# A four-layer graph network on one core: unit and group bases by PE, key preparation ahead of the squares, a two-table start of twelve groups, and node phases with table rows by ACT

## The reference, cut to what matters

```python
def _L0_gnn_ref(x, rows, cols, vals):               # layer 0: hyperbolic weighted mean
    x_hyp = expmap0(x, C)
    x_hyp_agg = weighted_midpoint_spmm(x_hyp, C, rows, cols, vals)
    return logmap0(x_hyp_agg, C)
...
x = _layernorm(x + _L0_gnn_ref(x, src, dst, edge_weight), axis=-1)
x = _layernorm(x + _L1_gnn_ref(x, src, dst, ...), axis=-1)   # conv, 64 experts top 2, batch norm
x = _layernorm(x + _L2_gnn_ref(x, src, dst), axis=-1)        # sum over edges, scaled by degrees
x = _layernorm(x + _L3_gnn_ref(x, edge_index, ...), axis=-1) # sum over edges, two matmuls, residual
```

## Time and profile before

| | us |
| --- | --- |
| median of 3 runs | 7333.98 |
| lowest and highest | 7331.43, 7337.74 |
| the profiled execution, its own time | 7343.66 |
| its span in the trace | 7342.10 |

### The profile page before, as it was taken

One profiled execution on the slowest core, in us unless ns is written; L12 is line 12 of the kernel. 1 busy time (PEld: TensorE's weight loads), 2 busy tenths in 40 slices (PEclk: granted clock), 3 DMA queues, 4 the chain that ended last, 5 costly groups with the idle time before them and its releaser, 6 DMA issues. The chain is left out here.

```text
span 7342.1 us, 132036 instructions
## 1 busy us (share of the span) xinstructions
PE 5009.0 (68%) x33175; PEld 3585.0 (49%) x33176; DVE 3839.1 (52%) x17654; ACT 1973.7 (27%) x5480; POOL 5243.1 (71%) x4321
## 2 busy tenths in 40 slices
PE   1666666666666677608998744951499995799985
PEld 1555555555555555505655433840265553565554
DVE  6776666777777777563242365322633325324225
ACT  1233334444444445332111001320311111211103
POOL 1788888888888888827777766147677776677774
PEclk6898888888888888659999856975699996899997
DMA  9677777777766777567775412741556563555553
GB/s 220 72 75 69 70 75 79 82 87 90 91 98 99 101 102 106 70 205 246 234 233 190 149 43 68 208 120 46 158 183 196 187 194 99 187 183 195 186 167 89
DMA packets 941947, 982.32 MB, mean 134 GB/s; under 512 B 203011, under 2 KB 824681, under 8 KB 941536
## 3 DMA queue, kind: packets, MB, share of 16 engines
q0 software_dynamic: 310624, 275.22, 29.3%
q1 hardware_dynamic: 284610, 520.71, 22.3%
q10 hardware_dynamic: 346302, 181.56, 8.6%
HBM read 622.06 MB, written 337.58 MB: 131 GB/s over the span
## 5 line engine op out<-in xcount | busy, mean ns | idle before, releaser
L793 POOL DMA_INDIRECT sums<-work,idx x1564 | 2467.9, 1578 | 624.0 <-issue 289.0
L760 POOL DMA_INDIRECT work<-table,src_t x2169 | 2184.6, 1007 | 684.8 <-issue 648.6
L1309 PE MATMUL pp<-shared 128*128 128x408 bf16 (+7 forms) x10584 | 1977.3, 342 | 325.1 <-DMA shared<-counts 204.4
L1309 PEld LDWEIGHTS pp<-shared 128*128 128x128 bf16 x10584 | 1020.8, 101 | 1126.6 <-issue 254.3
L1743 DVE TENSOR_TENSOR acc<-acc,pp 128x80 f32 x543 | 129.3, 238 | 1440.1 <-PE pp L1291 1419.0
L1291 PE MATMUL pp<-work 128*128 128x80 f32 x4338 | 630.0, 293 | 366.3 <-DMA work<-table,src_t 222.1
L1291 PEld LDWEIGHTS pp<-work 128*128 128x128 f32 x4338 | 592.0, 207 | 493.6 <-DMA work<-table,src_t 316.6
L1206 PE MATMUL pp<-acc 128*128 128x130 f32 x3128 | 548.9, 329 | 348.0 <-ACT work L957 348.0
L1206 PEld LDWEIGHTS pp<-acc 128*128 128x128 f32 x3128 | 481.2, 234 | 366.5 <-issue 366.5
L957 ACT ACTIVATE work<-pp 128x520 f32<-128x520 f32 x391 | 236.2, 604 | 1272.8 <-DMA sums<-work,idx 1262.0
L974 ACT ACTIVATE shared<-pp 128x441 bf16<-128x441 f32 (+18 forms) x1086 | 547.2, 550 | 114.0 <-PE pp L1245 80.0
(11 more groups left out here) (328 smaller groups left out, 6924.1 us busy)
## 6 DMA issues: line engine op xcount, KB each, us to landing
shared<-counts SPq DMA_DIRECT2D x84, 840.0 KB
shared<-counts SPq DMA_DIRECT2D x42, 882.0 KB
work<-table,src_t POOLq DMA_INDIRECT x2169
shared<-counts SPq DMA_DIRECT2D x42, 819.0 KB
shared<-counts SPq DMA_DIRECT2D x42, 808.5 KB
shared<-counts SPq DMA_DIRECT2D x42, 798.0 KB
shared<-counts SPq DMA_DIRECT2D x42, 756.0 KB
shared<-counts SPq DMA_DIRECT2D x42, 714.0 KB
```

The costliest lines, as they stand in the source:

```text
L760: pool.indirect_dma_start(out=msg[:, i % SLOTS, k, :], out_offset=None, in_=table, in_offset=bass.IndirectOffsetOnAxis(ap=src_t[:, at:at + ...
L793: pool.indirect_dma_start(out=sums0[table], out_offset=bass.IndirectOffsetOnAxis(ap=picked, axis=0), in_=rows, in_offset=None, bounds_chec ...
L1309: i = pe.matmul(bank[c][:, 0:COLS[n]].rearrange("p (k w) -> p k w", w=PACK * w), x3[:, b % 2, h, part3, :], ring[:, q % RING, 0:TB * COLS[ ...
```

## The change

**Bases by PE.** Eight matmuls with `g_min` or `h_min`, broadcast, against the identity spread the bases over all partitions in PSUM, ahead of the transposes; DVE copies them to `base_bc` and `ubase_bc` and from there to the two rows. Five of POOL's twelve number DMAs and four of its six loads go.

```diff
+            pe.wait_ge(prep, 3)
+            for q in range(NQ):
+                m = P if q < NQ - 1 else GREST
+                pe.matmul(bases_ps[:, q * P:q * P + m], g_min[0:m, q:q + 1].to_broadcast([m, P]), ident[0:m, 0:m], start=True, stop=True)
+            for n, (q, h) in enumerate(((0, 0), (0, 1), (1, 0), (1, 1))):
+                i = pe.matmul(ubases_ps[:, n, :], h_min[:, q, h:h + 1].to_broadcast([P, P]), ident[:, :], start=True, stop=True)
+            i.then_inc(w_pe, 1)
             pe.wait_ge(srcf_ready, 2)
...
+            dve.wait_ge(w_pe, 1)
+            dve.tensor_copy(base_bc, bases_ps[:, 0:NG])
+            dve.tensor_copy(ubase_bc[:, 0:WHOLE], ubases_ps[:, 0, 0:WHOLE])
...
+            dve.tensor_copy(base_row[:, :], base_bc[0:1, :])
+            dve.tensor_copy(unit_base, ubase_bc[0:1, :]).then_inc(unit_step, 1)
```

```diff
+            act.wait_ge(x_in, 16 * (NB + 1))
+            act.wait_ge(x_pad, 1)
             act.wait_ge(pool_const, 2)
             clear_sums0(act, 0, 0, (NT + 1) // 3, sums_zero)
-            act.wait_ge(x_in, 16 * (NB + 1))
-            act.wait_ge(x_pad, 1)
```

```diff
-        PIECES0 = [(NT + 1) // 3 * n // SLOTS for n in range(SLOTS + 1)]
+        PAIRED = APART * SLOTS
+        PIECES0 = [(NT + 1) // 3 * n // PAIRED for n in range(PAIRED + 1)]
...
-                first = isinstance(g, int) and g < SLOTS
+                first = isinstance(g, int) and g < PAIRED
```

```diff
+            def scaled_rows(layer):
+                def body(b, s, turn):
+                    apart(act, x_ready, layer * NB + b + 1)
+                    act.wait_ge(tab_stored[s], 16 * ((layer + 1) * STORES + turn))
+                    for j in range(TB):
+                        i = act.activation(slot[:, 2 + s, j, :], X[:, b * TB + j, :], ACT.Copy,
+                                           scale=in_scale[:, layer, ds(b * TB + j, 1)])
+                    i.then_inc(tab_ready, 1)
...
-            batches(pool, shift, scale_rows(1, 1), lags=(0, 1))
+            batches(pool, shift)
...
-            batches(act, normal_rows(1, 0), deviation(1), lags=(1, 0))
+            batches(act, normal_rows(1, 0), deviation(1), scaled_rows(1), lags=(1, 0, 1))
...
-            batches(act, hidden3, turned3, deviation(3), normal_rows(3, 2), store_out, lags=(1, 0, 2, 3, 3))
+            batches(act, hidden3, turned3, normal_rows(3, 2), store_out, deviation(3), lags=(1, 0, 3, 3, 2))
...
-            batches(dve, normal(1), residual1, lags=(1, 0))
+            batches(dve, residual1, normal(1), moments(1, 0), lags=(0, 1, 0))
...
-            batches(dve, stage2, normal(2), residual2, lags=(0, 2, 1))
+            batches(dve, stage2, residual2, normal(2), moments(2, 0), lags=(0, 1, 2, 1))
```

More of the change, by code:

```diff
@@ L440, in rounds @@
                     body(turn * SLOTS + s, s, turn)
+            for turn in range(APART):
+                whole(turn)
+            with eng.Fori(APART, TURNS - 1) as turn:
+                whole(turn)
+            whole(TURNS - 1)
+            whole(TURNS, range(1))
         def spans(eng, body):
@@ L829, in _ @@
             extra_windows(pool, scatter_extra)
-            batches(pool, scale_rows(0, 0))
             gather(1)
@@ new lines, in _ @@
+            dve.tensor_scalar(bits_hi, src_t[:, :], -P, None, ALU.bitwise_and).then_inc(bits_ready, 1)
+            dve.wait_ge(bits_ready, 4)
+            dve.wait_ge(key_step, 1)
+            dve.tensor_copy(low_key, bits_lo[:, 0:NKEY])
+            for n in range(len(SPANS)):
+                of = slice(C0[n], C0[n + 1])
+                dve.tensor_scalar(past_key[:, of], key[:, of], float(WIDTH[n]), MASKED, ALU.is_ge, ALU.mult)
+                i = dve.scalar_tensor_tensor(key[:, of], bits_hi[:, of], WIDTH[n] / P, key[:, of], ALU.mult, ALU.add)
@@ L1621, in _ @@
-            dve.wait_ge(bits_ready, 5)
-            dve.scalar_tensor_tensor(dst_n, bits_lo, float(NT), dst_n, ALU.mult, ALU.add).then_inc(bits_ready, 1)
-            dve.wait_ge(bits_ready, 6)
-            dve.tensor_scalar(less_dump, dst_n, col[:, 6:7], None, ALU.subtract).then_inc(bits_ready, 1)
-            dve.wait_ge(bits_ready, 7)
-            with dve.Fori(1, NB // 2) as i:
-                for half in range(2):
-                    table0_rows(2 * i + half, half, i)
-            dve.wait_ge(weights_in, 9 * 16)
@@ L1934, in residual0 @@
                 i.then_inc(y_ready, 1)
-                moments(0, 0)(b, s, turn)
-            batches(dve, normal(0), residual0, lags=(1, 0))
+            batches(dve, residual0, normal(0), moments(0, 0), lags=(0, 1, 0))
             sums(1)
```

187 lines of the change are left out of this document (80 added, 107 removed).

## The result

The changed kernel takes 7324.06 us at the median of 20 runs (7316.23 to 7330.55), the kernel before 7334.59 of 20 beside it (7322.19 to 7340.20). The ratio is 0.9986 with an interval from 0.998 to 0.9992: 10.5 us less, between 6 and 15. The forecast was 7312, 22 us less; the time lies in its range, and the gain is half of what was forecast. The change is 0.14 per cent, less than the 0.2 that the forecast took for no change, to which it gave 0.31. Its range, 7294 to 7348, also holds the time of the kernel before, so a time inside it says little for the mechanism. The two traces therefore differ by 23.6 us, and 13 of these are no effect that the medians show. So the stages are compared one by one.

What follows compares the result with a forecast made beforehand. Bound by POOL's unbroken scatter-adds in layer 0, started late by clears and table stores, and by DVE-ACT chains in the node phases. Terms -12.5 + 4 - 11 + 2.5 - 5 = -22 give 7312 us from median 7333.98; range 7294 to 7348.

Steps and rivals of the forecast that it cites:

- Prologue: Before layer 0's scatter-adds: fewer base writes and earlier clears start the third table batch sooner; -11 us (-4 to -14).
- ACT's clear no longer shares that stretch with x: Prologue: with writes also gone, x ends at 37 us (34 to 44) in place of 48.22.
- Twelve groups: Layer 0's start, twelve groups on two tables: halved clears against six more paired groups; -1.5 us (-9 to +8).
- The first scatter-add 4 us sooner behind the first window: Layer 0's two-table phase: half the clearing load lets POOL's first scatter-add follow the first window 4 us sooner.
- Node phase 0: ACT makes table rows and DVE's new order lengthens the period from 5.01 to 5.28 us; +4 us (0 to +9).
- The ring: Node phase 0's cycle: rows of X, a later batch's residual, `normal`, rows of X again; 5.28 us per batch.
- Node phase 1: POOL no longer holds up DVE's offset; period 5.57 us in place of 6.43; -11 us (-14 to -5).
- Node phase 2: DVE's new order gives a period of 5.28 us in place of 5.09; +2.5 us (0 to +4).
- Node phase 3: Residual no longer waits, PE limits; period 6.0 us in place of 6.28, shorter end; -5 us (-8 to 0).
- The lock: Node phases 1 to 3: POOL's product starts first and holds DVE's offset 2.1 us; 7348 or 7372 us; chance 0.22.
- Rival 2: Prologue and two-table phase gain little: 7323 or 7321.5 us, both together 7332.5; chance 0.25 in its forms.
- its second form: Two-table phase: SP runs some eight windows ahead, first groups still take 20 us; +8 in place of -1.5; 7321.5 us.

Runs made afterwards that it cites:

- the node phases alone: Kernel before with only the changed kernel's edits of the four node phases, front as before; ratio 0.9997 (0.9988 to 1.0006).
- the fill ahead of x: Changed kernel with ACT's clear of table 0 put back ahead of its wait for x; ratio 0.9991 (0.9982 to 1.0) to the kernel before.
- the probe: Changed kernel with a 128x128 DVE copy between residual and reciprocal in node phase 1, delaying the offset behind POOL's start; one execution, 7379.68 us.

## Why the prediction was half right

- **Prologue, -11 forecast, -9.9 measured at the first scatter-add.** The size was right, and two of the edits make it. The removed writes gain 6 to 8 us. "ACT's clear no longer shares that stretch with x" gains too, but not by the third batch, which began at the same time with the clear ahead of x again: it gains by the later of the two clears and the second store. That the keys are hidden behind the clearing was right, and it means that their move was worth nothing. X was complete at 42.9 and not at 37: without the clear the DMA engines were at 0.88 of their time with 105 GB/s from 30 to 40 us, no more bytes than in the same stretch of the earlier trace rows. The writes show in such stretches by their rate: with the clear beside x, 113 GB/s with them (the node phases alone) and 158 without (the fill ahead of x).
- **Twelve groups, -1.5 forecast, +2.4 measured on the first chip and about +6 to +8 on the others.** The forecast counted from the first window, where the prologue is 9.5 us earlier and this stretch 2.0 longer; the sum is the same. Two terms of the sum were mis-sized. "The first scatter-add 4 us sooner behind the first window" did not happen: 15.3 us in place of 15.7. And the eight later groups took 75.8 us in place of 73.6, 9.5 each in place of 9.2. The first four took 51.2, better than the 54 of the sum. The upper bound of +8 held, the sign was wrong.
- **Node phase 0, +4 forecast, +7.7 measured.** The ring was read rightly but mis-sized, 5.45 in place of 5.28: from the end of the rows of X (3264.81) to the residual (3265.07) 0.26 us pass and not 0.12, from the offset to ACT 0.23 and not 0.13. And a step is missing: in the new order the first offset also waits for the second residual, so that the first rows of X come 2.23 us behind the first root and not 0.86.
- **Node phase 1, -11 forecast, -8.2 measured.** The period was right (5.63 against 5.57), though of what made it 6.43 before only the held offset was read, and not the held residual L2137. The missing step is the same. In the kernel before, ACT's first root and its first rows of X:

```profile
5146.36 0.30 ACT L1047 ACTIVATE sd<-mv,col 128x7 f32<-128x7 f32 x1 [11.19 <-DVE mv L1860]
5147.22 2.80 ACT L1055 ACTIVATE X<-work,off,sd 128x128 f32<-128x128 f32 x7 [0.57 <-DVE off L1870]
```

and in the changed kernel:

```profile
5139.88 0.30 ACT L1021 ACTIVATE sd<-mv,col 128x7 f32<-128x7 f32 x1 [11.19 <-DVE mv L1860]
5142.44 2.80 ACT L1029 ACTIVATE X<-work,off,sd 128x128 f32<-128x128 f32 x7 [2.26 <-DVE off L1870]
```

  The idle time ahead of the rows of X grows from 0.57 to 2.26: a sum over 13 periods does not see what stands ahead of the first. The forecast took the two edits of this phase together, too. ACT's rows in the old order gain 14 us, and the new order then gives 6 back.
- **Node phase 2, +2.5 forecast, +3.5 measured:** the period's part is 1.6 (5.22 against 5.09, over 13), the rest the same late start, 1.8.
- **Node phase 3, -5 forecast, -6.3 measured.** Period 5.88, where PE's 5.9 of the earlier trace rows was taken as the limit. The chain that ended last agrees. Its shares by line from 7254 to 7325 before, and from 7235 to 7300 now:

```profile
by line: ACT X L1055 35.1%; DVE w_t L1856 22.7%; DVE work L2179 17.1%; issue 11.0%; DVE mv L1860 8.3%; ACTq L1055 4.1%; ACT sd L1047 0.7%; DVEq L2178 0.6%; DVEq L394 0.3%; ACTq L1146 0.2%; ACTq L394 0.2%
```

```profile
by line: PE pp L1452 30.6%; PE pp L1453 26.1%; PE pp L1442 23.4%; ACT shared L1126 15.6%; issue 4.8%
```

  It now runs through PE, 80 per cent, and through ACT's activation between two of PE's steps (L1126 in `hidden3`).
- **Sum:** -22 forecast, -10.8 measured in the stretches that the change touches. The difference is 3.9 in the two-table phase, 7.5 in node phases 0 to 2, 1.1 in the prologue, less 1.3 in phase 3.
- **The rivals.** The lock did not come: the offset keeps 167 ns at the mean in all 14 batches of phase 1, at a margin of 0.04 to 0.07 us in eleven of them; the forecast's 0.20 less 0.14 is 0.06. Its price is about what the earlier trace rows said, 1.80: with its start 0.09 on the other side the offset takes 2.00. The Trainium skill, "SBUF — State Buffer", section "Who interferes with whom", lets the order of issue decide who blocks; the probe agrees, 2.00 against 0.17 us. Rival 2, the front that gives little, holds in large part on the other chips, by its second form: the two-table phase costs most of what the prologue gains. The first group took 16 to 19 us there and not 20, but SP did run ahead: in the changed kernel the clears behind eight windows were issued from 134.9 to 164.0, when POOL had reached its second group.

## What to carry to other kernels

A period times the number of batches is not the price of a reordered loop: read what stands ahead of the first batch as well, since whatever is put between a result and its user delays the first use once and in full. When two edits of one stage are made together, cost each without the other; here one gained 14 us and the other then lost 6, and only a kernel with one of them showed it. A transfer of few bytes in single elements, issued while a large load runs, can cost as much as a large clear beside the same load (6 to 8 us and 5 here). And a row that comes at the same time in two kernels does not clear an edit: here the third batch did, and the fourth was 4 us late.

## What the runs showed of the hardware

- 763 elements of 4 bytes, written one by one from many partitions while x was loading, moved the first scatter-add by 6 to 8 us (163.1 against 156.8 and 155.0).
- Two clears of 6435 KB landed 28.0 and 59.1 us after their issue from one queue, 44.8 and 50.2 from two. The first table store landed at 90.8 with both clears in another queue and at 94.4 with one of them in its own; the second store landed just behind the later clear wherever one clear was served ahead of the other (99.7 behind 99.5, and 99.2 behind 99.0).
- The same instructions differ by chip and by execution: 379 groups of scatter-adds 2848 to 2864 us, the experts 831 to 842, the twelve paired groups 127 on one chip and 133 to 138 on the others. A difference of a few us between two traces is read only in the stretches that an edit touches.
- An offset of 0.17 us ahead of POOL's product by 0.04 us was held up in no batch; behind it by 0.09 us it lasted 2.00. A residual with two operands from SBUF, 1.08 us alone, took 2.77 behind the start of the same product.
